# Attention row sums from pairs that an accumulating DMA joins, read four steps behind the exponentials

## The reference, cut to what matters

```
scores = jnp.einsum('bhqd,bhkd->bhqk', Q, K) / scale
scores = jnp.where(m, jnp.float32(-1000000000.0), scores)
attn = jax.nn.softmax(scores, axis=-1)
ctx = jnp.einsum('bhqk,bhkd->bhqd', attn, V)
```

## Time and profile before

| | |
|---|---|
| runs shown | 1577.43, 1582.28, 1584.48 us; median 1582.28 us |
| profiled execution | 1579.47 us, its span 1577.7 us |
| TensorE clock granted, mean | 0.964 of full speed |
| busy share of the span: PE, DVE, POOL, ACT | 89%, 82%, 59%, 55% |
| attention, first to last start of an exponential | 351.1 to 1153.1 us |

### The profile page before, as it was taken

One profiled execution on the slowest core, in us unless ns is written; L12 is line 12 of the kernel. 1 busy time (PEld: TensorE's weight loads), 2 busy tenths in 40 slices (PEclk: granted clock), 3 DMA queues, 4 the chain that ended last, 5 costly groups with the idle time before them and its releaser, 6 DMA issues. The chain is left out here.

```text
span 1577.7 us, 34377 instructions
## 1 busy us (share of the span) xinstructions
PE 1402.0 (89%) x14575; PEld 579.6 (37%) x14598; DVE 1291.7 (82%) x1337; ACT 868.2 (55%) x932; POOL 930.1 (59%) x693
## 2 busy tenths in 40 slices
PE   3899999659999999999999999999969839893997
PEld 1344444313333333333333333333324314441443
DVE  7777776388888888888888888888529969999786
ACT  3233323216666666667766767666732458763453
POOL 7222111028888888888888888888936669900000
PEclk9899999889999999999999999999989959996999
DMA  9466555570332133312332133300038506653986
GB/s 293 114 225 214 181 179 192 135 203 9 85 81 66 35 85 88 79 38 65 86 82 62 39 85 82 85 22 13 21 120 277 202 27 255 249 217 113 335 291 220
DMA packets 126921, 207.06 MB, mean 131 GB/s; under 512 B 11956, under 2 KB 65204, under 8 KB 125248
## 3 DMA queue, kind: packets, MB, share of 16 engines
q1 hardware_dynamic: 119616, 187.73, 38.6%
q0 software_dynamic: 3424, 8.95, 1.8%
q10 hardware_dynamic: 3744, 8.39, 1.5%
HBM read 124.29 MB, written 72.35 MB: 125 GB/s over the span
## 5 line engine op out<-in xcount | busy, mean ns | idle before, releaser
L718 POOL TENSOR_TENSOR x<-x 128x512 f32<-128x512 f32 x512 | 673.6, 1328 | 141.3 <-ACT x L759 134.9
L786 DVE TENSOR_REDUCE row_max<-ring 128x1 f32<-128x1024 f32 x512 | 609.9, 1214 | 99.5 <-PE ring L620 97.5
L759 ACT ACTIVATE x<-ring 128x1024 f32<-128x1024 f32 x512 | 514.1, 1024 | 240.5 <-PE ring L682 239.5
L644 PE MATMUL o_acc<-x,v 128*32 128x512 f32 x2048 | 264.4, 592 | 3.2 <-ACT x L759 2.3
L682 PE MATMUL ring<-ffn_w_int 128*32 128x512 f16 x2560 | 194.2, 380 | 6.0 <-DVE row_max L786 6.0
L620 PE MATMUL ring<-ffn_w_int 128*32 128x512 f16 x2560 | 193.8, 379 | 6.1 <-DVE row_max L786 6.1
L620 PE MATMUL ring<-x 128*32 128x512 f16 x1536 | 119.2, 392 | 26.9 <-DMA v<-scratch_V 15.5
L653 PE MATMUL sum_acc<-x,ones 128*32 128x512 f32 x1024 | 132.1, 592 | 1.5 <-POOL x L718 1.5
L1146 PE MATMUL hid<-xqT,ffn_w_int 128*128 128x512 bf16 x499 | 119.6, 394 | 10.2 <-ACT xqT L1176 8.0
L1355 PE MATMUL down<-ffn_w_int,hq 128*128 128x512 bf16 x502 | 113.4, 383 | 15.2 <-ACT hq L1341 14.5
L682 PE MATMUL ring<-x 128*32 128x512 f16 x1536 | 115.4, 380 | 4.2 <-DVE row_max L786 4.1
(11 more groups left out here) (181 smaller groups left out, 2063.9 us busy)
## 6 DMA issues: line engine op xcount, KB each, us to landing
scratch_G<-gelu SPq DMA_DIRECT2D x56, 512.0 KB, 2.6
g_in<-scratch_G SPq DMA_DIRECT2D x28, 1024.0 KB, 5.9
x<-in_ctxT SPq DMA_DIRECT2D x8, 1024.0 KB, 6.9
x<-in_x SPq DMA_DIRECT2D x8, 1024.0 KB, 8.8
scratch_V<-x SPq DMA_DIRECT2D x32, 256.0 KB, 3.1
v<-scratch_V SPq DMA_DIRECT2D x16, 512.0 KB, 8.5
out<-x POOLq DMA_DIRECT2D x7, 1024.0 KB, 7.3
ffn_w_int<-scratch_QH SPq DMA_DIRECT2D x20, 256.0 KB, 4.1
```

What stands on the lines that cost most here:

```text
L644: last = nc.tensor.matmul(oacc[h * DK:(h + 1) * DK], v[buf][:, kt, h * DK:(h + 1) * DK], prob[:, s % 2, h, part], tile_position=(0, h * DK ...
L718: nc.gpsimd.tensor_tensor(pair[:, s % 2, h], prob[:, s % 2, h, 0], prob[:, s % 2, h, 1], ALU.add).then_inc(pair_done, 1)
L759: nc.scalar.activation(prob[:, s % 2, h], ring[slot][:], ACT.Exp, scale=SM_SCALE).then_inc(exp_done, 1)
L786: nc.vector.tensor_reduce(mraw[:, i:i + 1], ring[slot][:], AX.XY, ALU.max).then_inc(max_done, 1)
```

## The change

Row sums are made once per two steps. POOL still makes a pair sum per head and step, now into six sets of pair buffers: the two of before, two in a new tile `pair_sums`, and two in the space of projection weights that are no longer needed (`w_hi`, `w_lo`). After every odd step POOL waits for its own last add and issues a DMA that adds the odd step's four pair sums (1 MB) to the even step's in place (`accum_op=ALU.add`). PE then multiplies the joined sums with ones once per two steps, in even steps alone, at the place of V2, for the steps four and three before (`LATE = 4`). The last two steps have no such DMA; their sums are multiplied one step at a time at the end.

The rest of the half's chain moves with the sums: `sums_out` goes from steps 1 and 5 to steps 3 and 7, `invert` and `normalize` from 2 and 6 to 0 and 4, `low` from 3 and 7 to 1 and 5, `high` likewise on ACT. The copy of `o_acc` gets a second buffer and stays where it was. The exponentials of a step now also wait until POOL has made the pair sums of two steps before.

```diff
-        pair = k.x2[:, 16:24].rearrange("p (s h) e -> p s h e", s=2)
+        PAIRS, LATE = 6, 4
+        QUADS = STEPS // 2
+        own_pairs = sb("pair_sums", [P, 2, GH, HALF], F32)
+        pair = [k.x2[:, 16 + GH * i:16 + GH * (i + 1)] for i in range(2)] + [own_pairs[:, i] for i in range(2)]
+        pair += [w[:, 0:2].rearrange("p i c e -> p (i c e)").bitcast(F32).rearrange("p (h e) -> p h e", h=GH) for w in (k.wh, k.wl)]
...
-        osum = sb("o_taken_out", [P, HALF], F32)
+        osum = sb("o_taken_out", [P, 2, HALF], F32)
...
+            def row_sums(quad, whole):
+
+                if whole:
+                    pe.wait_ge(quad_done[quad % (PAIRS // 2)], 16 * (quad // (PAIRS // 2) + 1))
+                else:
+                    pe.wait_ge(pair_done, 2 * GH * (quad + 1))
+                if quad % (KP // 2) == 0:
+                    pe.wait_ge(sums_taken, quad // (KP // 2))
+                for step in range(2 * quad, 2 * quad + (1 if whole else 2)):
                     for h in range(GH):
-                        last = nc.tensor.matmul(dacc[h * DK:(h + 1) * DK], k.ones[:], pair[:, s % 2, h],
-                                                tile_position=(0, h * DK), start=(kp == 0), stop=(kp == KP - 1))
-                    last.then_inc(pv_done, 1)
+                        last = nc.tensor.matmul(dacc[h * DK:(h + 1) * DK], k.ones[:], pair[step % PAIRS][:, h], tile_position=(0, h * DK),
+                                                start=(step % KP == 0), stop=(step % KP + (2 if whole else 1) == KP))
+                last.then_inc(sums_done, 1)
...
                         s, part = i
+                        if part == 2:
+                            late = STEPS * t + s + 1 - LATE
+                            if late >= 0 and late % 2 == 0:
+                                row_sums(late // 2, True)
+                            continue
...
                     pool.wait_ge(exp_done, SU * (t + 1) + i + 1)
-                    nc.gpsimd.tensor_tensor(pair[:, s % 2, h], prob[:, s % 2, h, 0], prob[:, s % 2, h, 1], ALU.add).then_inc(pair_done, 1)
+                    if h == 0 and n >= PAIRS:
+                        pool.wait_ge(sums_done, (n - PAIRS) // 2 + 1)
+                    nc.gpsimd.tensor_tensor(pair[n % PAIRS][:, h], prob[:, s % 2, h, 0], prob[:, s % 2, h, 1], ALU.add).then_inc(pair_done, 1)
+                    if h == GH - 1 and n % 2 and n < STEPS * GROUPS - 1:
+                        quad = n // 2
+                        pool.wait_ge(pair_done, GH * (n + 1))
+                        pool.dma_start(pair[(n - 1) % PAIRS], pair[n % PAIRS], accum_op=ALU.add).then_inc(quad_done[quad % (PAIRS // 2)], 16)
...
                             act.wait_ge(pv_done, STEPS * (t + 1) + s + 1)
+                            if STEPS * t + s >= 2:
+                                act.wait_ge(pair_done, GH * (STEPS * t + s - 1))
...
-            AFTER = {(1, 0): sums_out, (2, 0): invert, (2, 2): normalize, (3, 2): low}
+            AFTER = {(3, 0): sums_out, (0, 0): invert, (0, 2): normalize, (1, 2): low}
```

More of the change, by code:

```diff
@@ L500, in stage_attend @@
         e_ready, x_turned, xt_copied = sem("minus_max_ready"), sem("minus_max_turned"), sem("max_rows_copied")
-        pv_done, o_summed, o_taken, sums_taken = sem("pv_done"), sem("o_summed"), sem("o_taken"), sem("sums_taken")
+        quad_done, sums_done = [sem(f"quad_summed{i}") for i in range(PAIRS // 2)], sem("sums_done")
+        pv_done, o_taken, sums_taken = sem("pv_done"), sem("o_taken"), sem("sums_taken")
         some_ready, rec_ready = sem("reciprocal_ready"), sem("reciprocal_rows_ready")
@@ L576, in body @@
                     load(t + 2, (buf + 2) % NB)
+                if not first:
+                    store(t - 1, 0)
                 max_rows(t, buf, 1)
@@ L581, in body @@
                     max_rows(t + 1, (buf + 1) % NB, 0)
-                store(t, 0)
             def store(t, hf):
@@ L595, in _ @@
             steps(sp, body)
+            store(GROUPS - 1, 0)
             store(GROUPS - 1, 1)
@@ L636, in product @@
                 hf, kp = divmod(s, KP)
[L637 to L642, removed]
-                    for h in range(GH):
[L644 to L652, removed]
-                        last = nc.tensor.matmul(dacc[h * DK:(h + 1) * DK], k.ones[:], pair[:, s % 2, h],
-                                                tile_position=(0, h * DK), start=(kp == 0), stop=(kp == KP - 1))
-                    last.then_inc(pv_done, 1)
+                kt = 2 * kp + part
@@ new lines, in product @@
+                if part == 0:
+                    pe.wait_ge(exp_done, SU * (t + 1) + GH * (s + 1))
+                    if kp == 0:
+                        pe.wait_ge(o_taken, 2 * t + hf)
+                for h in range(GH):
+                    last = nc.tensor.matmul(oacc[h * DK:(h + 1) * DK], v[buf][:, kt, h * DK:(h + 1) * DK], prob[:, s % 2, h, part],
+                                            tile_position=(0, h * DK), start=(kt == 0), stop=(kt == KT - 1))
+                if part == 1:
+                    last.then_inc(pv_done, 1)
@@ L708, in _ @@
             steps(pe, body)
-            for part in range(3):
+            for part in range(2):
                 product(STEPS - 1, part, GROUPS - 1, (GROUPS - 1) % NB)
+            for quad in range(QUADS * GROUPS - LATE // 2, QUADS * GROUPS):
+                row_sums(quad, quad < QUADS * GROUPS - 1)
         @block.gpsimd
@@ L734, in take_out @@
                 n = 2 * t + hf
-                act.wait_ge(on_ready, n + 1)
-                act.wait_ge(o_summed, n + 1)
-                nc.scalar.copy(osum[:], oacc[:]).then_inc(o_taken, 1)
+                act.wait_ge(on_ready, n)
+                act.wait_ge(pv_done, STEPS + 2 + STEPS * t + (hf + 1) * KP)
+                nc.scalar.copy(osum[:, hf], oacc[:]).then_inc(o_taken, 1)
             def high(hf, t):
@@ L763, in body @@
                             take_out(1, t - 1)
-                        if (s, h) == (KP + 3, 0):
-                            high(0, t)
-                        if (s, h) == (3, 0) and not first:
+                        if (s, h) == (1, 0) and not first:
+                            high(0, t - 1)
+                        if (s, h) == (KP + 1, 0) and not first:
                             high(1, t - 1)
@@ L778, in _ @@
             take_out(1, GROUPS - 1)
-            high(1, GROUPS - 1)
+            for hf in range(2):
+                high(hf, GROUPS - 1)
         @block.vector
@@ L796, in sums_out @@
                 n = 2 * t + hf
-                dve.wait_ge(pv_done, STEPS + 2 + STEPS * t + (hf + 1) * KP)
+                dve.wait_ge(sums_done, (n + 1) * KP // 2)
                 nc.vector.transpose(sums[:].rearrange("p b j -> p (b j)"), dacc[:]).then_inc(sums_taken, 1)
@@ L812, in normalize @@
                 dve.wait_ge(oh_ready, n)
-                nc.vector.tensor_tensor(on[:], osum[:], rec[:], ALU.mult).then_inc(on_ready, 1)
+                nc.vector.tensor_tensor(on[:], osum[:, hf], rec[:], ALU.mult).then_inc(on_ready, 1)
             def low(hf, t):
@@ L842, in body @@
                             piece = AFTER[s % KP, m - 1]
-                            if s >= KP:
+                            if s == STEPS - 1:
                                 piece(0, t)
                             elif not first:
-                                piece(1, t - 1)
+                                piece(int(s >= KP - 1), t - 1)
             dve.sem_inc(x_turned, 2)
@@ L855, in _ @@
             steps(dve, body)
+            for piece in (invert, normalize, low):
+                piece(0, GROUPS - 1)
             for piece in (sums_out, invert, normalize, low):
```

1 line of the change is left out of this document (added).

## The result

The changed kernel takes 1629.6 us (median of 4 runs, 1627.1 to 1631.8) where the kernel before takes 1581.7 (1577.4 to 1584.5). The ratio is 1.030, 95% interval 1.028 to 1.032: slower by 3.0%, where I had forecast 1565 and a gain. The profiled execution has a span of 1625.3 us.

A forecast was written before the change was run, and what follows sets the result against it. PE was taken to bound the kernel, DVE not far behind. 30 halves x 0.66 gave 20 us gained, less 4 lost at the end: -16 against 1579.5, so 1563.5, forecast as 1565, range 1543 to 1598 us.

The forecast's parts named there:

- What POOL takes on: POOL's adds 21.2 us a half plus two DMAs, 3.0 us: 24.2, just below the new half of 24.8.
- the walk: Step-by-step timing of one half in the new order: PE waits 2.61 us, so a half takes 25.27 us.
- the walk's step 4: Even step with `invert` and `normalize` (0.78 us) on DVE; PE's S3 waits 0.29 us.
- The ring takes some of it back: PE's ring waits return part of the removed 1.71 us a half; half taken as 24.8, gain 0.66.
- DVE takes it all: Rival: chain pieces on DVE meet the shortened odd step; half 25.3 to 26.0, 1579 to 1600 us; chance 0.22.
- The hold: Time each accumulating DMA occupies POOL: 0.90 us taken, 0.6 to 1.3 expected in the profile.
- the wait before it: POOL's wait for its own last add before each DMA: 0.60 us taken.
- Landing: Accumulating DMA, issue to arrival: 8 to 10 us, covered by 15.2 us until PE's V2 needs it.
- the engines' share: Load on the 16 DMA engines: 0.26 to 0.77 added to today's 0.29, 0.80 in all at two moves.
- The clock: Sign in the profile after: the granted clock still 1.00.
- the last group: End of the stage, where nothing covers POOL's DMAs and one more row-sum set is needed: 4 us lost.
- a group of 51 us or more: Sign that would disprove the forecast; `sums_out` starts were expected 49.6 us apart by group.

The follow-up runs named there:

- kernel 2: The changed kernel without the accumulating DMA and POOL's wait for it, row sums reading the odd steps' pair sums alone: 1580.9 us, ratio 0.999.
- kernel 9: The changed kernel with joined row sums one step later and `sums_out`, `invert`, `normalize` all in steps 0 and 4: 1624.3 us, ratio 1.026.
- kernel 10: kernel 9 with the reciprocal rows in PSUM instead of SBUF, the next row sums waiting for `normalize`: 1581.2 us, ratio 0.999.
- kernel 8: kernel 2 with DVE's reductions over the second half of the keys only: 1527.0 us, ratio 0.965.
- kernel 6: kernel 5 without the DMA, row sums reading the odd steps' pair sums alone: 1577.7 us, ratio 0.997.
- kernel 4: The kernel before with POOL's wait and a 1 MB accumulating DMA between spare buffers added after each odd step: 1598.8 us, ratio 1.011.
- kernel 7: The changed kernel with POOL also waiting for `normalize` before the last add of steps 0 and 4: 1594.1 us, ratio 1.008.
- kernel 3: The changed kernel without the DMA, PE summing both steps' pair sums in the even step: 1620.1 us, ratio 1.024.
- kernel 5: The changed kernel, DMAs kept, with joined row sums split by columns, 256 of 512 in each step, and the chain spread: 1594.2 us, ratio 1.009.

## Why the prediction was wrong

**The step that failed first** is in "What POOL takes on": POOL's adds at 41.65/50 x 25.46, "contention with DVE included". I took the contention as a fixed cost inside POOL's own durations and asked only who waits for POOL's semaphore. Nobody does, much (ACT's exponentials as forecast stay nearly covered). But DVE waits for POOL's adds without a semaphore: `normalize`, a term of 0.78 in the walk's step 4, read from a row in which POOL paused beside it, took 2.97 in the run of adds behind the DMA. I had both halves of it, that POOL would be set back after each odd step (1.5 us taken, 1.17 measured) and that `invert` and `normalize` move to the following even step, and didn't put them together. That adds behind a DMA overlap, and let nothing with two SBUF inputs in between, no row of the kernel before could show. Measured price: 26.96 - 25.35 = 1.61 us a half between the changed kernel and kernel 2, 48 us, all of it in PE's waits before an S (3.20 us a half against 1.59). None of my rivals names it. The Trainium skill does: "SBUF — State Buffer", section "Who interferes with whom", says that a DVE instruction with two SBUF inputs contends with a GpSimd instruction that reads SBUF, and one with at most one SBUF input, outside the 2-port performance modes, doesn't. Kernels 9 and 10 agree, 2.17 against 0.67 us; I didn't weigh that rule.

**The second** is the scaling in "The ring takes some of it back". The walk gave new waits of 2.61 us, a half of 25.27; I scaled them by 1.09/1.44 and took 24.8. Kernel 2, the change as the walk saw it, has 25.35, with waits of 2.67. The walk was right in its total and the correction wrong: an error of 1.09 against 1.44 in the old order is no factor for waits that stand elsewhere. Part of that agreement is luck, since `normalize` takes 1.36 in kernel 2 and not 0.78, and one wait of 0.31 is not in the walk. PE's gain is eaten by waits in the ring: in kernel 2 1.85 us a half before an S or the turn, nearly all for DVE, and 0.82 before an M, for ACT. The half is that of the rival "DVE takes it all" (25.3 to 26.0), to which I gave 0.22; its mechanism is the larger part of the cause, not all of it, as kernel 8 shows.

The two add up: 30 x (0.55 + 1.61) = 65 us, and the result is 1629.6 - 1565 = 65 us off. That they meet so closely is luck: 30 x 1.50 = 45 us stands for a measured 40.5, and the last group lost 5.6 us, not 4.

**What held.** 520 matmul rows of row sums and 63 DMAs. The hold, 0.87 us (0.90 taken); the wait before it, 0.30 (0.60). Landing in 7.9 us (8 to 10), covered by the window; the engines' share 0.69 (0.55 to 1.06 by the bounds). The clock. Two smaller terms were off: the last group lost 5.6 us, where 4 was taken, and POOL was busy 84% of the window, not 97%.

**What I named as its disproof** came true in one point, a group of 51 us or more (53.9); the two points I worried about, the transfer and the DMA's hold, didn't.

**Open**: why POOL's adds overlap behind a DMA, and how much of the 2.6 to 2.7 us that kernels 2, 6 and 10 still lack to PE's work is the reductions' length and how much the order in the ring. `low` also has two SBUF inputs and waited up to 8.3 us in kernel 4's last group; a form with one in PSUM wasn't tried.

## What to carry to other kernels

Before moving work to an engine's idle time, ask who lives in that idle time: here VectorE's `normalize`, with two SBUF inputs, got in between GpSimd's adds until a DMA of GpSimd's stood ahead of them, and that cost 43 us (kernels 9 and 10) to 48 us (the changed kernel and kernel 2). If such an instruction has to stand there, put one of its inputs in PSUM, or let GpSimd wait for it once. And an engine that is busy for 97% of a stretch need not be worth relieving: relieve the 89% one in a trial (halve its work) and see which moves the half.

## What was not expected of the hardware

- `normalize` doesn't get in between two adds of POOL in a run that begins behind a DMA of POOL's: it waited for the end of a run of four (2.97 us), and in the last group 7.9 us. In kernel 7, with a pause after three, 1.73. In runs without a DMA ahead it mostly waits for one add: 0.92 and 1.30 us in the last group of the kernel before, a median of 1.36 in kernels 2 and 3. The longest exception is a `low` of 6.5 us in the last group of kernel 6.
- With one input in PSUM it takes 0.67 us beside the same adds, no slower than with both in SBUF and POOL idle (0.69, the last one of the stage).
- An accumulating DMA of 1 MB lands in 7.9 us (6.9 to 14.0). The Trainium skill's fit ("DMA: Bandwidth & Descriptors", section "Anatomy of one DMA") with two reads of 1 MB, in the prediction, is 6.8 by estimate: the quickest agrees, the median is 1.1 us above. The software queue went from 28 to 356 us of the 16 engines for 66 MB more: 5.0 us per accumulated MB against 3.2 for a moved one.
- Beside these DMAs small transfers land late: the 32 KB of `max_rows` in 4.8 us (median) in the changed kernel and up to 6.0 in kernel 5, where they take 1.9 before and in kernels 3 and 6, without the DMAs.
